# Taking the last score sum of a batch off VectorE: ScalarE copies the scores, GpSimd adds them

## What is computed

```python
dots = jnp.einsum('bnsq,bntq->bnst', qq, kq)
fid = dots / jnp.maximum(qn[..., :, None] * kn[..., None, :], EPS_COS)
qw = fid * (1.0 + 0.1 * jnp.sin(fid * jnp.pi))
cw = jnp.einsum('bnsd,bntd->bnst', Q, K) / np.sqrt(HD).astype(np.float32)
aw = RATIO * qw + (1.0 - RATIO) * cw
probs = jax.nn.softmax(aw, axis=-1)
heads = jnp.einsum('bnst,bntd->bnsd', probs, V)
```

## Time and profile before

| what | value |
|---|---|
| runs | 564.98, 566.42, 568.71 us (median 566.42) |
| the profiled execution | 564.39 us, span 562.3 us |
| DVE busy over the span | 405.7 us (72%) |
| PE busy | 370.2 us (66%) |
| ACT busy | 340.4 us (61%) |
| POOL busy | 257.7 us (46%) |
| mean granted TensorE clock | 0.861 |
| L1691 (`logits`), 64 instructions | 76.3 us busy, 1211 ns each |

### The profile page before, as it was taken

One profiled execution on the slowest core, in us unless ns is written; L12 is line 12 of the kernel. 1 busy time (PEld: TensorE's weight loads), 2 busy tenths in 40 slices (PEclk: granted clock), 3 DMA queues, 4 the chain that ended last, 5 costly groups with the idle time before them and its releaser, 6 DMA issues.

```text
span 562.3 us, 8513 instructions
## 1 busy us (share of the span) xinstructions
PE 370.2 (66%) x2408; PEld 249.2 (44%) x2408; DVE 405.7 (72%) x934; ACT 340.4 (61%) x698; POOL 257.7 (46%) x387
## 2 busy tenths in 40 slices
PE   0959427787777887788776779770000099999970
PEld 0744215554444554454443333560000088888850
DVE  4896828699999999999999924469880017666771
ACT  0334234389988889888897845775300177777740
POOL 8463013134444444444440112245477406777874
PEclk9999957689999889988997799985555589999995
DMA  9370202245555455455554499900011314767600
GB/s 215 19 166 3 56 6 59 57 118 146 129 124 137 121 128 137 107 138 129 134 132 97 75 145 140 246 1 1 19 44 53 95 41 127 205 191 199 176 18 0
DMA packets 81243, 58.16 MB, mean 103 GB/s; under 512 B 17619, under 2 KB 72919, under 8 KB 81196
## 3 DMA queue, kind: packets, MB, share of 16 engines
q1 hardware_dynamic: 75142, 53.12, 42.3%
q0 software_dynamic: 2496, 4.29, 2.3%
q10 hardware_dynamic: 3558, 0.20, 0.5%
HBM read 35.38 MB, written 23.11 MB: 104 GB/s over the span
## 4 chain that ended last, share of the span: by engine, by line
DVE 38%; issue 22%; PE 20%; SPq 8%; DMA 4%; POOL 3%; ACT 2%; ACTq 1%; POOLq 0%; DVEq 0%
DVE mxs L1591 11%; DVE big L1691 10%; DVE big L1663 8%; PE ps L1431 7%; PE ps L1442 6%; SPq L502 4%; SPq L541 3%; DVE gb L1505 2%; DMA x_all<-sorted_rows 1%; POOL out_dram L767 1%; DMA bc2q_row<-in_L_attn_bc2q_dram 1%; PE ps L1259 1%; PE ps L1451 1%; PE ps L1246 1%; DMA qk_parts<-proj 1%
## 5 line engine op out<-in xcount | busy, mean ns | idle before, releaser
L1663 DVE SCALAR_TENSOR_TENSOR big<-big,ps 128x1024 f32<-128x1024 f32 x64 | 74.5, 1215 | 13.7 <-ACT big L866 13.7
L1691 DVE SCALAR_TENSOR_TENSOR big<-big,ps 128x1024 f32<-128x1024 f32 x64 | 76.3, 1211 | 7.9 <-PE ps L1259 7.8
L1591 DVE TENSOR_REDUCE mxs<-ps 128x4 f32<-128x1024 f32 x64 | 76.4, 1216 | 1.1 <-PE ps L1131 1.1
L870 ACT ACTIVATE big<-big 128x1024 f32<-128x1024 f32 x64 | 66.1, 1053 | 11.5 <-DVE big L1691 11.3
L1246 PE MATMUL ps<-proj 128*128 128x256 f16 x256 | 43.9, 304 | 35.4 <-DVE mxs L1591 22.3
L866 ACT ACTIVATE big<-ps 128x1024 f32<-128x1024 f32 x64 | 63.6, 1015 | 2.9 <-PE ps L1246 2.5
L1983 DVE TENSOR_SCALAR arena<-ps,x_all 128x128 f32<-128x128 f32 x46 | 14.0, 346 | 65.6 <-PE ps L1451 55.9
L767 POOL DMA_INDIRECT out_dram<-arena,fidx x46 | 46.8, 1018 | 17.8 <-issue 17.5
L681 POOL CAST mtok<-mxs 128x8 bf16<-128x8 f32 x32 | 6.1, 191 | 104.8 <-DVE mxs L1591 104.8
L1021 ACT ACTIVATE x_all<-x_all 128x128 f32<-128x128 f32 x46 | 20.2, 489 | 55.1 <-DMA x_all<-sorted_rows 54.8
L1259 PE MATMUL ps<-arena 98*128 98x256 bf16 x256 | 42.3, 293 | 10.3 <-DVE big L1663 7.8
(11 more groups left out here) (314 smaller groups left out, 881.1 us busy)
## 6 DMA issues: line engine op xcount, KB each, us to landing
big<-in_L_ffn_w_dram SPq DMA_DIRECT2D x46, 256.0 KB
qk_parts<-proj SPq DMA_DIRECT2D x16, 384.0 KB, 3.0
arena<-qk_parts SPq DMA_DIRECT2D x32, 192.0 KB, 3.5
sorted_rows<-zrow SPq DMA_DIRECT2D x16, 266.0 KB, 3.7
arena<-qk_parts SPq DMA_DIRECT2D x32, 128.0 KB, 3.9
proj<-u_parts SPq DMA_DIRECT2D x48, 64.0 KB
x_all<-sorted_rows SPq DMA_DIRECT2D x23, 133.0 KB
sorted_rows<-zrow SPq DMA_DIRECT2D x2, 1263.5 KB, 24.3
```

The lines of the kernel that those rows point to most:

```text
L870: nc.scalar.activation(W[par1][:, n, :], W[par1][:, n, :], ACT.Exp).then_inc(p_ready, 1)
L1591: nc.vector.tensor_reduce(mxs[:, b1 % 2, :, 2 * n:2 * n + 2], src, AX_X, ALU.max, negate=True).then_inc(unit_free, 1)
L1663: nc.vector.scalar_tensor_tensor(W[par][:, n, :], W[par][:, n, :], 10.0, f, ALU.add, ALU.mult).then_inc(unit_free, 1)
L1691: nc.vector.scalar_tensor_tensor(W[par][:, n, :], W[par][:, n, :], 0.05, slot_of("log", b, n), ALU.mult, ALU.add).then_inc(unit_free, 1)
```

## The change

`logits(3)` leaves DVE. In its place ACT copies `log` 3 out of PSUM, times 20, into an SBUF tile `score` (`take_score`, between `take_max(b+1, 0)` and `exp(b, 2)`), and POOL adds `score` to W as the last step of its batch (`add_score`). `exp(b, 3)`, which stands in the list of the next batch behind its `take_qk`, waits for that sum and applies the factor 0.05 itself. `score` uses a part of `late_s` that is free at this time. The slot of `log` 3 is freed by `score_out` in place of `unit_free`, so PE waits for ACT there ahead of `cos` 0 of the next batch; `freed(k)` counts the units that DVE still frees.

```diff
+        score = late_s[:, 0:UW]
...
+        def freed(k):
+            return sum(1 for kind, b, n in units[:k + 1] if (kind, n) != ("log", HP - 1))
...
             def split_max(b, r):
-                pool.wait_ge(unit_free, unit_no["max", b, 2 * r + 1] + 1)
+                pool.wait_ge(unit_free, freed(unit_no["max", b, 2 * r + 1]))
...
+            def add_score(b, par):
+                pool.wait_ge(score_out, b + 1)
+                pool.wait_ge(unit_free, freed(unit_no["cos", b, HP - 1]))
+                w = W[par][:, HP - 1, :]
+                nc.gpsimd.tensor_tensor(w, w, score, ALU.add).then_inc(score_in, 1)
...
                 nc.gpsimd.tensor_tensor(xb, xb, mv_all[:, 0, b * TPB:(b + 1) * TPB].unsqueeze(2).to_broadcast([P, TPB, C]), ALU.subtract)
+                add_score(b, par)
...
                 def exp(b1, par1, n):
-                    act.wait_ge(unit_free, unit_no["log", b1, n] + 1)
-                    nc.scalar.activation(W[par1][:, n, :], W[par1][:, n, :], ACT.Exp).then_inc(p_ready, 1)
+                    last_unit = n == HP - 1
+                    if last_unit:
+                        act.wait_ge(score_in, b1 + 1)
+                    else:
+                        act.wait_ge(unit_free, freed(unit_no["log", b1, n]))
+                    nc.scalar.activation(W[par1][:, n, :], W[par1][:, n, :], ACT.Exp, scale=0.05 if last_unit else 1.0).then_inc(p_ready, 1)
+
+                def take_score():
+                    act.wait_ge(unit_ready, unit_no["log", b, HP - 1] + 1)
+                    if not first:
+                        act.wait_ge(score_in, b)
+                    nc.scalar.activation(score, slot_of("log", b, HP - 1), ACT.Copy, scale=20.0).then_inc(score_out, 1)
...
                 for n in range(HP - 1):
+                    if n == HP - 2:
+                        take_score()
                     exp(b, par, n)
...
+            def slot_free(k):
+                if k >= 3:
+                    kind, b0, n = units[k - 3]
+                    if (kind, n) == ("log", HP - 1):
+                        pe.wait_ge(score_out, b0 + 1)
+                    else:
+                        pe.wait_ge(unit_free, freed(k - 3))
...
                 logits(2)
                 if first:
                     weights_3()
-                logits(3)
                 if not first:
                     heads(b - 1)
```

More of the change, by code:

```diff
@@ L300, in bass_sandwich @@
         unit_free = sem("unit_free")
+        score_out = sem("score_out")
+        score_in = sem("score_in")
         sin_ready = sem("sin_ready")
@@ L1133, in max_unit @@
                 mm.then_inc(unit_ready, 1)
+            def slot_free(k):
[5 more added lines that the diff above has]
+                        pe.wait_ge(unit_free, freed(k - 3))
             def unit(kind, b1, n):
                 k = unit_no[kind, b1, n]
-                if k >= 3:
-                    pe.wait_ge(unit_free, k - 2)
+                slot_free(k)
                 return slot[k % 3]
```

## The result

| | median us | lowest to highest | runs |
|---|---|---|---|
| before | 564.98 | 564.04 to 568.71 | 7 |
| changed | 572.97 | 571.52 to 575.70 | 7 |

The ratio is 1.0138, 95% interval 1.0107 to 1.0168: the change makes the kernel about 1.4% slower. The forecast was 573.0 us; the median is 572.97. That the two agree so closely is luck. The forecast added 6.6 us to a median before of 566.42, from three runs; over seven runs that median is 564.98, and the change cost 8.0 us. The start was 1.4 us too high and the cost 1.4 us too low. Within the cost, two more errors cancel in part: the steps of the loop cost less than forecast, and the end of the attention more.

The account below looks back on a forecast made before the run. DVE was taken as full at 14.24 us a batch, with the loop through ACT next at 13.76. Terms 3.7 + 0.6 + 0.4 + 1.9 = +6.6 us on the 566.42 us median gave 573.0 us; range 566.5 to 578.5.

Parts of the forecast that it names:

- the loop through ACT: Waits from first `weight` via `top`, `take_max`, `exp(b, 2)`, table load and `sin(0)` to next `weight`: 13.76 us against DVE's 14.24.
- The copy costs 0.92: ACT's `take_score`, between `take_max` and `exp(b, 2)`, lengthens the loop from 13.76 to 14.68 us, +0.44 us per batch.
- The sum is covered: POOL's add of 2.26 us per batch (at most 2.47) costs nothing unless it takes over 3.2 us.
- `cos` 0 is covered: PE's next-batch `cos` 0 waits for the copy, which ends about 2.3 us before `sin(0)`; `cos` 0 takes 0.6.
- The 13 steps from batch 1 to 14: Attention batches: 187.1 us before, 190.8 at the loop's pace, +3.7 us; +0.6 (0 to 2.0) for kept waits.
- The step to batch 15: The step into the last attention batch, forecast to be 0.4 us longer.
- The end costs 1.9 us: Last batch has no cover for POOL's sum: attention ends 1.6 to 2.4 us later, and all that follows waits.
- The median stands 2.0 us above the profiled execution: Whole kernel before: profiled execution 564.39 us, median of three runs 566.42; the 2.0 us were added to reach 573.0.
- the bounds as stated: Forecast's spread: 5.7 to 8.5 us by the waits and the end, +3 by a dearer copy; 571 to 578 us.
- the rival with two table loads: ACT reloads its table for the scaled copy, two 1.28 us loads per batch: +36, 602 us; chance 0.10 with other slower cases.

Follow-up runs that it names:

- e2: The kernel before without `logits(3)`, and with no copy or sum in its place (last unit's scores left out); 554.64 us, ratio 0.9790.
- e1: The kernel before plus one ScalarE copy per batch that nobody reads, `logits(3)` kept on VectorE; 569.05 us, ratio 1.0047.
- e3: The changed kernel without GpSimd's sum, the copy kept in its place; 567.10 us, ratio 1.0082.
- e9: The changed kernel with GpSimd's sum done twice, with half the scores each time; 597.37 us, ratio 1.0564.
- e11: The changed kernel run once more, unedited; 572.98 us, ratio 1.0136.
- e12: The changed kernel with `logits(3)` of the last batch alone back on VectorE, no copy or sum there; 568.06 us, ratio 1.0052.
- e4: The changed kernel with the copy one place earlier, ahead of `take_max(b+1, 0)`; 563.29 us, ratio 0.9970.
- e7: The changed kernel with the copy ahead of `take_max(b+1, 0)` and `exp(b, 2)` moved into the next batch; 560.21 us, ratio 0.9926.

## Why the prediction was right, point by point

- **DVE is full, and the loop through ACT has 0.48 us of slack**: right. With the instruction gone and nothing added, the step fell by 0.51 (e2).
- **The removed instruction is not in the loop**: right. DVE's 1.13 us came back in gaps of 0.37 and 1.03 us.
- **The copy costs 0.92 and is in the loop; step 14.68**: right, 0.92 and 14.64; e1 has 14.68 with the copy alone.
- **The sum is covered, up to about 3.2 us**: right for one sum (e3) and for two (e9), and its price of 2.35 us lay between the bounds. In one batch the sum ends at 214.16 us, and `top(b+1, 3)` at 214.02, so a longer sum would hold up `split_max` at once; by e9 the step would still bear about 0.9 us of that.
- **`cos` 0 is covered though its slot comes free with the copy**: right. From 125 to 300 us PE never waits for the copy in the changed kernel, and the steps of e1 and of the changed kernel differ by 0.04 only, though one of them frees the slot as before.
- **The 13 steps from batch 1 to 14 cost 3.7 + 0.6 us**: 6.5 in the first profile (193.5 against 187.0), which is of the slowest of the seven runs, 575.70 us, and 4.5 in the second (e11). By the ratios of e1 and e12, which have the loop's loss without the end's, all that is not the end costs less: 0.5%, some 3 us, as in both the last batch is 1.1 us shorter than before. The size of this term stays uncertain by 2 us, since the waits in batches with a low clock differ from run to run. The step to batch 15 was 15.3 us against 15.7, not 0.4 longer.
- **The end costs 1.9 us and all that follows only waits for it**: this is the term that was mis-sized. Against the kernel before, the last batch's own part looks right: 17.65 against 16.08 us, so 1.6. Against e12, whose last batch is 15.0 us, copy and sum cost 2.65 there; as the step ahead of it was 0.5 longer in e12, 2.1 us are left of the two together. And what follows does not only wait: the middle stage of the changed kernel was 4.5 us longer than before and 3.5 longer than in e12, with PE at the low clock as it began. Forecast 1.9; e12 against e11 gives 0.8%, 4.7 us.
- **The median stands 2.0 us above the profiled execution**: over seven runs it stands 0.6 above it. The forecast of 573.0 us rests on this term as much as on the 6.6 us; with 564.98 as its start the same sum gives 571.6.
- Two sums beside the forecast don't come out. With the bounds as stated (5.7 to 11.5 us over 566.4) the lower end is 572, not 571; and the rival with two table loads, counted from the forecast like its neighbour, is 609 us, not 602.

So of about 8 us, some 3 are the loop's and some 5 the end's, where the forecast had 4.7 and 1.9. Both mechanisms were in it; the second was priced at its direct length alone. The Trainium skill ("Perfetto Trace Analysis", Identifying the Most-Contended Engine) says to optimise the engine with the highest occupancy first. e2 agrees: taking work off VectorE gained 0.51 us a batch. It gained no more, and the changed kernel lost, because the next bound was a chain, which the occupancy of no engine shows.

## What to carry to other kernels

Before work is taken from a full engine, add up the loops of waits that run through the others: the distance to the longest of them is all that the change can win, and what it adds in that loop beyond this distance is paid in full, however idle its engine looks. When work must go on such an engine, its place in the order counts as much as its length (0.59 us a batch for moving one instruction by one place, 0.95 for taking another out of the loop). Treat the last round of a pipeline apart: there is little behind which an added step can hide, and a TensorE left idle there can take a low clock into the next stage.

## What the hardware showed beyond that

An idle gap of 1.86 us on TensorE at the end of a stage was followed by matmuls at 1.81 in place of 1.07 us, by a granted clock of 0.70 over the first 10 us of the next stage, and by a stage 3.5 to 4.5 us longer, in both profiles of the changed kernel. There the gap's own length was the smaller part of the price. In e4 and e7, with the same gap and clocks of 0.72 and 0.75, the next stage was only about 1 us longer, so the price of such a gap is not fixed.
